# Row maximum of an attention kernel taken in twelve one-bank parts instead of eight, joined by a small maximum

## The reference

```
sim = jnp.einsum('bhid,bhjd->bhij', q, k)
sim = jnp.where(causal_mask, mask_value, sim)
attn = jax.nn.softmax(sim, axis=-1)
out = jnp.einsum('bhij,bhjd->bhid', attn, v)
...
return out @ w_out
```

## Time and profile before

| | |
|---|---|
| median of 3 runs | 1455.18 us (1453.99 to 1457.58) |
| the profiled execution's own time | 1456.36 us |
| its span in the profile | 1454.6 us |
| busy over the span | PE 94%, DVE 76%, ACT 72%, POOL 65% |
| attention phase | from about 269 us of the span |
| a round of eight heads (863.84 to 1009.01 us) | 145.17 us |

### The profile page before, as it was taken

The page is one execution under the profiler, slowest core; times in us unless marked ns, Lnnn a source line. Parts: engine busy times, 40 slices in busy tenths (PEclk is TensorE's granted clock), DMA queues, the critical chain, the costliest instruction groups (busy, mean ns, idle before and its releaser), DMA issues.

```text
span 1454.6 us, 26818 instructions
## 1 busy us (share of the span) xinstructions
PE 1368.9 (94%) x8618; PEld 1022.5 (70%) x8618; DVE 1101.0 (76%) x1928; ACT 1053.4 (72%) x2589; POOL 941.4 (65%) x933
## 2 busy tenths in 40 slices
PE   3689999699999999999999999999999999999996
PEld 3579998467767676777677767676767676767674
DVE  6645555469886988698869886988698869886974
ACT  2556666377778777877787778777877787778774
POOL 0774000278667866786677668766876687668775
PEclk9789999699999999999999999999999999999998
DMA  9122221122212221222122212221222122212122
GB/s 333 64 88 74 67 63 51 37 58 50 50 45 63 50 51 45 63 50 51 45 63 50 51 45 63 50 50 46 63 50 51 45 65 49 50 45 64 49 45 77
DMA packets 77225, 89.87 MB, mean 62 GB/s; under 512 B 17656, under 2 KB 54816, under 8 KB 77088
## 3 DMA queue, kind: packets, MB, share of 16 engines
q1 hardware_dynamic: 59168, 69.90, 19.2%
q10 hardware_dynamic: 13824, 9.86, 2.2%
q0 software_dynamic: 4096, 8.40, 2.0%
HBM read 37.25 MB, written 16.78 MB: 37 GB/s over the span
## 4 chain that ended last, share of the span: by engine, by line
PE 51%; DVE 21%; POOL 5%; issue 2%; ACT 1%; DMA 1%; POOLq 0%; SPq 0%; ACTq 0%
PE max_ps L1273 8%; DVE row_max L1125 7%; PE score_ps L1298 6%; PE score_ps L1299 6%; PE head_ps L1326 6%; PE head_ps L1315 6%; PE head_ps L1317 6%; PE misc_ps L1336 3%; POOL p_lo L1039 3%; DVE x_row L1138 3%; DVE q_a L1115 3%; PE misc_ps L1249 2%; DVE k_b L1115 2%; DVE heads L1180 2%; PE max_ps L1276 2%
## 5 line engine op out<-in xcount | busy, mean ns | idle before, releaser
L1039 POOL TENSOR_TENSOR p_lo<-probs,p_hi 128x512 fp32r<-128x512 f32 (+3 forms) x768 | 797.3, 1057 | 308.6 <-ACT p_hi L1077 304.6
L1077 ACT ACTIVATE probs<-score_ps 128x512 f32<-128x512 f32 (+3 forms) x768 | 376.8, 491 | 180.6 <-PE score_ps L1301 99.7
L1125 DVE TENSOR_REDUCE row_max<-max_ps 128x1 f32<-128x128 f32 (+7 forms) x512 | 385.2, 754 | 159.8 <-PE max_ps L1276 155.0
L1077 ACT ACTIVATE p_hi<-score_ps 128x512 fp32r<-128x512 f32 (+3 forms) x768 | 376.0, 490 | 0.0
L1298 PE MATMUL score_ps<-q_a,k_a 128*128 128x512 f32 (+3 forms) x768 | 287.5, 374 | 3.1 <-DMA q_b<-shift 2.5
L1326 PE MATMUL head_ps<-p_lo,v_hi 128*65 128x512 f32 (+3 forms) x768 | 275.9, 359 | 1.0 <-POOL p_lo L1039 1.0
L1315 PE MATMUL head_ps<-p_hi,v_hi 128*65 128x512 f32 (+3 forms) x768 | 275.0, 358 | 0.0
L1299 PE MATMUL score_ps<-q_b,k_b 65*128 65x512 f32 (+3 forms) x768 | 268.0, 349 | 0.0
L1317 PE MATMUL head_ps<-p_hi,v_lo 128*64 128x512 f32 (+3 forms) x768 | 259.0, 337 | 0.0
L1273 PE MATMUL max_ps<-k_a,q_a 128*128 128x384 f32 (+5 forms) x768 | 232.5, 357 | 24.4 <-DVE row_max L1125 19.0
L1273 PEld LDWEIGHTS max_ps<-k_a,q_a 128*128 128x128 f32 x768 | 131.6, 191 | 76.6 <-DVE row_max L1125 43.4
(11 more groups left out here) (162 smaller groups left out, 2172.1 us busy)
## 6 DMA issues: line engine op xcount, KB each, us to landing
k_a<-k_a SPq DMA_DIRECT2D x64, 256.0 KB, 3.6
q_b<-q_a SPq DMA_DIRECT2D x64, 256.0 KB, 4.4
scale<-inv_rows SPq DMA_DIRECT2D x128, 128.0 KB, 2.9
sorted_x<-zeros SPq DMA_DIRECT2D x13, 384.0 KB, 15.9
sorted_y<-result ACTq DMA_DIRECT2D x78, 64.0 KB
w_raw<-sorted_x SPq DMA_DIRECT2D x25, 192.0 KB
acc<-in_L_attn_x_dram SPq DMA_DIRECT2D x4, 512.0 KB, 7.4
w_raw<-in_L_ffn_W_dram ACTq DMA_DIRECT2D x1, 2048.0 KB, 23.2
```

What stands on the lines that cost most here:

```text
L1039: pool.tensor_tensor(p_lo[:, slot, 0:w], probs[:, n_chunk(g, c) % PROBS, 0:w], p_hi[:, slot, 0:w].bitcast(F32), ALU.subtract).then_inc(p_s ...
L1077: ins = act.activation(p[:, n_chunk(g, c) % ring, 0:width], score_ps[n_chunk(g, c) % 2][:, 0:width], ACT.Exp, scale=SCALE)
L1125: dve.tensor_reduce(row_max[:, g % 2, t:t + 1], src, axes, ALU.max).then_inc(max_taken, 1)
```

## The change

Each wide part is split in two parts of one bank each, so there are twelve parts (`max_parts`: tile, first key, width, and whether it touches the diagonal). Parts use the two banks in turn, and part `m` waits for the reduction of part `m - 2` alone. The second half's maximum goes to a column of its own (`row_max` has 12 columns), and after the last part one `tensor_tensor` maximum joins 4 columns with 4 (merge, L1130 of the changed kernel); the second shift waits for it by a new semaphore. Parts now stand in every chunk from c0 (parts 0 and 1) to c10 (part 11). The third projection unit moves from c3 to c4 and the sixth from c10 to c9, the combine steps from c4 and c6 to c3 and c7, and the second output projection of a pair from c10 to c5 of the odd head; the last combine step waits for the additions before it.

```
-            row_max = sb(ph2, "row_max", [P, 2, TILES])
+            row_max = sb(ph2, "row_max", [P, 2, TILES + GROUP])
...
-            max_parts = [(0, 0), (1, 1), (2, 0), (3, 1), (7, None), (6, None), (5, None), (4, None)]
-            MAX_AT = [0, 1, 2, 3, 5, 7, 10, 11]
-            FIRST_WIDE = {0: (4, 5), 1: (6,), 2: (7,)}
...
+            max_parts = [(t, 0, (t + 1) * P, True) for t in range(4)]
+            for t in (7, 6, 5, 4):
+                w = (t + 1) * P // 2
+                max_parts += [(t, 0, w, False), (t, w, w, True)]
+            MAX_AT = {0: (0, 1)}
+            MAX_AT.update({c: (c + 1,) for c in range(1, CH - 1)})
+            FIRST_WIDE = {0: (4, 5, 6), 1: (7, 8, 9), 2: (10, 11)}
...
-            PROJECT_AT = [{1: 0, 2: 1, 3: 2, 5: 3, 6: 4, 10: 5}, {}]
+            PROJECT_AT = [{1: 0, 2: 1, 4: 2, 5: 3, 6: 4, 9: 5}, {}]
...
-            COMBINE_AT = [(g, c) for g in (3, 4, 5, 6, 7) for c in (0, 1, 4, 6, 8, 9, 10, 11)][:COMBINE_STEPS]
-            Y_AT = {11: 0, 22: 1}
+            COMBINE_AT = [(g, c) for g in (3, 4, 5, 6, 7) for c in (0, 1, 3, 7, 8, 9, 10, 11)][:COMBINE_STEPS]
+            Y_AT = {11: 0, 17: 1}
...
                     def maximum(g, m):
-                        t, bank = max_parts[m]
+                        t, k0, w, _ = max_parts[m]
+                        to = t + GROUP if k0 else t
                         dve.wait_ge(max_scores, n_max(g, m) + 1)
...
+                        dve.tensor_reduce(row_max[:, g % 2, to:to + 1], max_ps[:, m % 2, 0:w], AX_X,
+                                          ALU.max).then_inc(max_taken, 1)
+                        if m == PARTS - 1:
+                            dve.wait_ge(max_taken, n_max(g, m) + 1)
+                            dve.tensor_tensor(row_max[:, g % 2, GROUP:TILES], row_max[:, g % 2, GROUP:TILES],
+                                              row_max[:, g % 2, TILES:TILES + GROUP], ALU.max).then_inc(max_merged, 1)
...
-                            pe.wait_ge(max_taken, n_max(g, BEFORE[m]) + 1)
...
+                            pe.wait_ge(max_taken, n_max(g, m) - 1)
+                        ins = pe.matmul(max_ps[:, m % 2, 0:w], q_a[i][s][:, t * P:(t + 1) * P],
+                                        k_a[i][s][:, k0:k0 + w], start=True, stop=not diagonal)
+                        if diagonal:
+                            ins = pe.matmul(max_ps[:, m % 2, w - P:w], later[:], ident16[:], start=False, stop=True)
```

More of the change, by code:

```diff
@@ L865, in beside @@
                 if g + 1 < ALL_HEADS and c in max_at:
-                    order.append(("max", g + 1, max_at.index(c)))
+                    order += [("max", g + 1, m) for m in max_at[c]]
                 if values:
@@ L906, in attention_and_experts @@
             order = [(kind, 0, n) for n in range(6) for kind in ("project", "project_lo")]
-            order += [("max", 0, m) for m in range(HALF_MAX[0] + 1)] + [("shift", 0, 0)]
+            order += [("max", 0, m) for m in range(NARROW)] + [("shift", 0, 0)]
             for at in range(ALL_HEADS * CH + 2 * CH):
```

35 lines of the change are left out of this document (13 added, 22 removed).

## The result

The changed kernel took 1516.47 us (median of 4 runs, 1515.25 to 1518.66), the kernel before 1455.94 us beside it on the same chip: a ratio of 1.0417, 95% interval 1.0399 to 1.0434. It is 61 us slower; 1440.0 was forecast, and the range ended at 1461.

A forecast was written before the change was run, and what follows sets the result against it. TensorE, 94% busy, was taken as the bound, waiting for VectorE's reductions. Terms -8.4 (places 3 to 5), -6.2 (place 6), -1.6 (first head) and +1.0 (neighbours) gave -15.2 us: 1441.2 profiled, 1440.0 as median, range 1424 to 1461.

The forecast's parts named there:

- What bounds the kernel: TensorE, busy 94% of the span, waits for VectorE's reductions of wide parts, which fill both banks.
- TensorE's neighbours: TensorE's matmuls stay the same but stand beside different ones; a cost of 1 us over the run, between 0 and 3.
- The merge at 0.46 us: VectorE's new maximum of two 128x4 SBUF inputs, priced at 0.46 us a head, between 0.15 and 1.35.
- has a chunk more of slack than before: The shift of c0 waits for the merge, but the last part now stands in c10, not c11.
- The rival "merge held": GpSimd holds VectorE's merge at 1.35 us each time, 1462 us in all; decides from 1.1 us a merge; chance 0.22.
- The combine steps stay the same in number: nothing: VectorE's combine steps, moved to other chunks of a head, were priced at no cost.
- Place 2's excess is GpSimd's and stays: Place 2, 0.70 us over its clean length while gathers keep GpSimd busy, was to stay unchanged.
- The splits: Four more VectorE reductions a head, 67 ns each behind cover, 0.27 us a head.
- The first rival: VectorE's busy time is stretched by holds that a freer order avoids; waits go altogether, 1424 us; chance 0.13.
- Unit 4 at nothing: Projection unit 4 in c6 needs the third projection's bank; 0.2 us left, priced at nothing where VectorE is on time.
- a sign of being wrong: Projection unit 4 waiting for VectorE in most even heads would show the forecast wrong.
- The first head (-1.6 us): The first head's waits of 1.32 and 0.62 us for two wide reductions nearly go with a bank free: -1.6 us.

The follow-up runs named there:

- e17: Changed kernel with merge as a one-input reduction, nine gathers moved to places 0 and 1, and combine steps spread anew over places 2 to 7; 1431.07 us, ratio 0.9825.
- e18: Kernel before (eight parts) with nine gathers moved to places 0 and 1 and the same combine-step placing as e17; 1444.49 us, ratio 0.9915.
- e3: Kernel before plus one two-input 128x4 maximum a head on spare columns, which the second shift waits for; 1508.78 us, ratio 1.0361.
- e1: Changed kernel with the merge as a reduction over pairs of columns, one SBUF input instead of two; 1479.71 us, ratio 1.0157.
- e5: Changed kernel with the old places for projections, combine steps and second output projection, merge untouched; 1474.45 us, ratio 1.0132.
- e9: Changed kernel with nine gathers moved earlier, to places 0 and 1, merge untouched; 1472.82 us, ratio 1.0112.
- e8: Changed kernel with the merge as a one-input reduction and the combine steps alone back at c4 and c6; 1463.24 us, ratio 1.0053.
- e7: Changed kernel with the merge as a one-input reduction and the projections alone back at c3 and c10; 1475.51 us, ratio 1.0139.
- e4: Kernel before (eight parts) with the changed kernel's places for projections, combine steps and second output projection; 1526.82 us, ratio 1.0493.
- e6: Changed kernel with the merge as a one-input reduction and old places for projections, combine steps and output projection; 1462.86 us, ratio 1.0057.
- e12: Kernel before with only the nine gathers moved earlier, to places 0 and 1; 1445.15 us, ratio 0.9923.

## Why the prediction was wrong

- **What bounds the kernel, and what the change is good for: right in kind.** TensorE waits for wide parts, and freeing a bank relieves it. With the holds and the backlog out of the way twelve parts are worth 13.4 us (e17 against e18); the sum had 16.2 for it and the first head, before the 1.0 for neighbours. That the two are close is luck: 1.7 us a round of the measured gain lie in places 7 and 2, where the prediction had nothing, and places 3 to 6 together give 0.6 where it had 1.9.
- **The merge at 0.46 us: the step that failed most.** It measured 1.07 in the mean, and the upper bound of 1.35, a hold of 1.26 and 0.09, was wrong in kind: the hold lasted 4.49 us behind a backlog, and 5.46 in e3. I took the longest L148 in the earlier trace rows as the longest hold, though those stand where GpSimd isn't behind, and priced the merge by one mean for all 64 instead of by the one in eight that stands behind the gathers. The earlier trace rows had the warning: GpSimd busy 19.47 of 20.56 us in place 2, right in front of the merge. That the shift "has a chunk more of slack than before" was true, and too little for 4.49 us. Worth 37 us (e1). This is no share of a sum: the old tables with the merge untouched take back 42 us (e5) and the early gathers 44 (e9), since each of them also shortens the hold.
- **The rival "merge held": right in mechanism and sign, a third of the size.** It gave 1462, worked out at 1.35 a merge, and said that 1.1 us decides. The mean was 1.066, just under that bar, and the time 61 us over: a bar on a mean is no test when one merge in eight takes 4.49 us and the others 0.58 in the mean. It also left out TensorE's clock, 0.52 for 3.4 us after the wait, which the waits alone don't show.
- **"The combine steps stay the same in number: nothing": wrong.** Moving them from c4 and c6 to c3 and c7 cost 16 us net (e8 against e1). Places 4 and 6 became 1.8 and 1.5 us longer by it, and place 7 became 1.4 shorter. The order of the instructions showed the move; I costed it by number alone.
- **"Place 2's excess is GpSimd's and stays": right on whose it is, wrong that it stays.** It grew by 1.36 us, 11 us in all. All twelve-part kernels with late gathers have it, with or without the merge (21.92 to 21.95, and 21.44 in e7), and with early gathers it goes (19.75 to 20.07), as long as no combine steps are put there. Why twelve parts make it longer was not settled: e4's tables do so with eight parts (21.40), e7's projection table takes a third of it back, and in e6 TensorE waits there for reductions (2.4 us) and not for `p_lo`, at the same length.
- **The splits: small, as forecast.** 256 more reductions took 30.7 us more busy time (415.9 against 385.2), 120 ns each before overlap, where the earlier trace rows gave 157 and the sum 67 behind cover. But VectorE's 15.99 us in place 3 were not work, as the sum took them: with early gathers the same 21 instructions are 12.21 us in the kernel before (e12), and place 3 of e1, e9 and e17 is 15.32 to 15.34 where 16.12 was forecast. The first rival's doubt was the better reading for that place.
- **Unit 4 at nothing: wrong as a wait, right as a price.** It waits 14.2 us in 17 of the 31 turns, up to 1.1, which was a sign of being wrong. But with the projection table put back (e7) only 1.6 us of it in 2 turns are left, and the waits of the weight loads for reductions rise instead, from 2.7 to 3.3 us in place 4 and from 2.2 to 2.9 in place 6, and neither place gets shorter.
- **TensorE's neighbours (1 us, 0 to 3): right.** Place 0 is 0.13 shorter, place 7 0.09 longer, and neither grew by 0.2.
- **The first head (-1.6 us): wrong.** 29.1 us against 29.0. With the old projection table alone it is 26.1 (e7), with the old combine table alone 28.6 (e8). The room was there, nearly twice what I forecast, and the new projection table took it: the step that I priced at nothing. Which of its two moves did so was not tested.
